# Attention scores with two stationary widths: 64 columns for the first 128 queries, 128 columns for the second

## What is computed

```
x = x + xattn(layernorm(x), ctx)          # x: 32 batches x 256 tokens x 256 features, ctx: 32 x 77 x 256
    q, k, v = heads(x @ Wq.T + bq), heads(y @ Wk.T + bk), heads(y @ Wv.T + bv)     # 8 heads of 32 features
    attn    = softmax(q @ k.T / sqrt(32) + causal)                                 # 256 x 77 per head
    out     = (attn @ v) @ Wo.T + bo
x = x + ffn(layernorm(x))
    h = silu(w1 x * s1) * (w2 x * s2);  h = gelu(h1 h * s);  h = gelu(h2 h * s);  out = w3 h * s   # 256 -> 1024 -> 1024 -> 1024 -> 256
```

## Time and profile before

| | |
|---|---|
| median of 3 runs | 1513.29 us (1512.74 to 1514.19) |
| the profiled execution | 1513.5 us, its span 1511.7 us |
| TensorE matmul busy | 1507.3 us (100% of the span), 8822 records |
| TensorE weight loads | 1201.6 us (79%) |
| VectorE / ScalarE / GpSimd | 841.7 us (56%) / 735.6 us (49%) / 115.1 us (8%) |
| granted TensorE clock | 1.000 |
| DMA | 92 GB/s mean |

### The profile page before, as it was taken

How to read it: one execution, slowest core, us unless ns; L and a number is a source line. 1 busy time by engine, 2 the same in 40 slices (tenths; PEclk the granted TensorE clock), 3 DMA queues, 4 the chain that set the end, 5 groups by cost and what they waited for, 6 DMA issues and landing times.

```text
span 1511.7 us, 22545 instructions
## 1 busy us (share of the span) xinstructions
PE 1507.3 (100%) x8822; PEld 1201.6 (79%) x8822; DVE 841.7 (56%) x1318; ACT 735.6 (49%) x1077; POOL 115.1 (8%) x119
## 2 busy tenths in 40 slices
PE   9999999999999999999999999999999999999999
PEld 6787887878878777887878878787887878878888
DVE  6754836458464564745548464574745648364432
ACT  5753635445363453635536364453634536354442
POOL 1001010010100101010010100101001010100000
PEclk9999999999999999999999999999999999999999
DMA  9962322233213222223223212322223223222100
GB/s 369 360 239 70 92 80 57 76 83 96 78 42 103 70 82 78 70 86 72 76 76 98 83 42 77 96 83 78 59 87 83 76 69 93 79 58 69 45 26 16
DMA packets 133747, 138.87 MB, mean 92 GB/s; under 512 B 74322, under 2 KB 105434, under 8 KB 130906
## 3 DMA queue, kind: packets, MB, share of 16 engines
q1 hardware_dynamic: 133722, 138.53, 30.4%
HBM read 78.70 MB, written 48.25 MB: 84 GB/s over the span
## 4 chain that ended last, share of the span: by engine, by line
PE 98%; DVE 1%; issue 0%; DMA 0%; SPq 0%; POOL 0%; DVEq 0%; POOLq 0%
PE ffn_banks L528 84%; PE att_banks L723 4%; PE att_banks L666 4%; PE att_banks L713 2%; PE att_banks L684 2%; PE ffn_banks L767 1%; PE ffn_banks L757 1%; PE ffn_banks L612 1%; DMA x_in<-in_x 0%; DVE a_f L970 0%; DVE probs L1030 0%; DVE a_lo L975 0%; PE att_banks L698 0%; PE att_banks L654 0%; DVE st L910 0%
## 5 line engine op out<-in xcount | busy, mean ns | idle before, releaser
L528 PE MATMUL ffn_banks<-b_hi,h_sb 128*128 128x512 f32 x1024 | 403.0, 394 | 0.0
L528 PE MATMUL ffn_banks<-b_lo,h_sb 128*128 128x512 f32 x1024 | 398.7, 389 | 0.0
L528 PE MATMUL ffn_banks<-a_hi,h_sb 128*128 128x512 f32 x1024 | 398.4, 389 | 0.0
L528 PE MATMUL ffn_banks<-a_lo,h_sb 128*128 128x512 f32 x1024 | 398.3, 389 | 0.0
L840 ACT ACTIVATE a_f<-ffn_banks,vec 128x512 f32<-128x512 f32 x128 | 88.3, 690 | 367.2 <-PE ffn_banks L528 367.2
L983 DVE TENSOR_TENSOR a_lo<-a_f,a_hi 128x512 fp32r<-128x512 f32 x128 | 103.9, 812 | 277.3 <-ACT a_hi L841 277.1
L528 PEld LDWEIGHTS ffn_banks<-b_hi,h_sb 128*128 128x128 f32 x1024 | 192.2, 188 | 45.6 <-issue 6.2
L528 PEld LDWEIGHTS ffn_banks<-a_hi,h_sb 128*128 128x128 f32 x1024 | 192.2, 188 | 39.9
L528 PEld LDWEIGHTS ffn_banks<-a_lo,h_sb 128*128 128x128 f32 x1024 | 192.2, 188 | 39.9
L528 PEld LDWEIGHTS ffn_banks<-b_lo,h_sb 128*128 128x128 f32 x1024 | 192.3, 188 | 39.4
L528 PE MATMUL ffn_banks<-ln_hi,w_sb 128*128 128x512 f32 x512 | 204.6, 400 | 0.4
(11 more groups left out here) (118 smaller groups left out, 1537.1 us busy)
## 6 DMA issues: line engine op xcount, KB each, us to landing
blocks_dram<-blocks SPq DMA_DIRECT2D x30, 512.0 KB, 3.1
attn_t<-blocks_dram SPq DMA_DIRECT2D x60, 256.0 KB
h_bits<-in_h SPq DMA_DIRECT2D x8, 1024.0 KB, 21.2
h_sb<-h_bits SPq DMA_DIRECT2D x8, 1024.0 KB, 9.9
x_in<-in_x SPq DMA_DIRECT2D x15, 512.0 KB, 3.6
ln_t<-in_x_t SPq DMA_DIRECT2D x15, 512.0 KB, 4.4
row_blocks_dram<-row_blocks SPq DMA_DIRECT2D x15, 512.0 KB, 4.1
row_blocks<-row_blocks_dram SPq DMA_DIRECT2D x60, 128.0 KB, 3.1
```

The lines of the kernel that those rows point to most:

```text
L528: mm = nc.tensor.matmul(psum, left, right, start=(k == 0 and part == 0), stop=(k == rows - 1 and part == 1))
```

## The change

`SCORE_COLS` becomes a pair, indexed by the half. The first 128 queries of a batch are scored as before, in 16 products of 64 stationary columns on eight tiles. The second 128 are scored in 8 products of 128 stationary columns, on four tiles of 32 rows by 128 columns. What is computed is the same.

```
-SCORE_COLS = 64
+SCORE_COLS = (64, 128)
...
                         for half in range(2):
                             for g in range(HG):
                                 at = half * G2 + g * TK
-                                for c in range(0, P, SCORE_COLS):
-                                    tokens = slice((2 * n + half) * P + c, (2 * n + half) * P + c + SCORE_COLS)
+                                for c in range(0, P, SCORE_COLS[half]):
+                                    tokens = slice((2 * n + half) * P + c, (2 * n + half) * P + c + SCORE_COLS[half])
                                     for h in range(4):
                                         rows = slice(HD * h, HD * (h + 1))
-                                        mm = nc.tensor.matmul(ab[c:c + SCORE_COLS, h, at:at + TK], q_t[rows, g, tokens],
+                                        mm = nc.tensor.matmul(ab[c:c + SCORE_COLS[half], h, at:at + TK], q_t[rows, g, tokens],
                                                               k_t[rows, g, n * TK:(n + 1) * TK], start=True, stop=True)
                         mm.then_inc(s_ready, 1)
```

## The result

The changed kernel takes 1515.85 us (median; 1515.31 to 1516.83) against 1512.95 us of the kernel before in the same runs: the ratio is 1.0018, 95% interval 1.0012 to 1.0024. The profiled execution has a span of 1513.7 us, against 1511.7.

The account below looks back on a forecast made before the run. TensorE, with a matmul under way 100% of the span, was taken as the bound. 32 score steps x 0.19 us = +6.1 us, other engines nothing, gave 1519.4 us against the median; range 1516.5 to 1521.5.

Parts of the forecast that it names:

- The first half: In each score step, the 16 products of 64 columns that are kept: 32 matmul records in 0.52 us.
- the switch: From 64 to 128 columns within a score step: array runs empty, first wide load 0.45 us after the step's start.
- the second half: Eight products of 128 columns on four tiles: loads in rounds 0.112 us apart, modelled end at 1.142 us.
- the end of the step: The product behind starts 0.07 us before the modelled end, at 1.07 against 0.89: 0.19 us more a step.
- The upper bound of the switch: Between 64 and 128 columns in a score step: the array runs empty; the lower bound was nothing.
- loads that wait for their own tile's stream: Rival, on the four wide tiles: a record takes 177 ns in place of 112; +12.3 us, 1525.8 us; chance 0.04.
- TensorE has no idle time to hide anything in: TensorE, 100% busy: whatever a score step gains or loses comes out of the total at full price, 32 times.
- item 4: ScalarE's copy and VectorE's mask behind S 0 have 2.2 us to spare, later products move back by 0.19: cost nothing.
- The last sentence: Sign of a wrong prediction: the step costs +0.19 us and the total doesn't follow, so TensorE had hidden slack.
- the first four cases: Slower by over 0.2%: forecast 0.79, no switch cost 0.09, load not hidden 0.04, loads in turn 0.01; given as 0.92.

Follow-up runs that it names:

- the kernel with three switches: The changed kernel with the width indexed by g, not the half (64, 128, 64, 128 in a step): 1526.91 us, ratio 1.0091 to the kernel before.

## Why the prediction was wrong

The direction was right; the size was not, and the fault lies outside the step.

- *The first half, the switch, the second half, the end of the step*: all held. 0.52, first wide load at 0.45, rounds of 0.112, product behind at 1.07, +0.184 against 0.19 forecast. The upper bound of the switch was the right end, and the kernel with three switches agrees with that price. So does the rule of the Trainium skill that the prediction set beside it ("TensorEngine Tiling (Array Packing)", "Key Properties"). No rival happened within the step: loads of a tile 0.112 apart leave no room for loads that wait for their own tile's stream, which would lie 0.177 apart.
- *"TensorE has no idle time to hide anything in"*, the first part's conclusion, is **the step that failed**. It took a matmul busy share of 100% for having no slack. A matmul's record lasts 0.39 while starts are 0.23 apart, so a wait of up to 0.16 between two products leaves no idle time in that row at all, and one of 0.25 hardly any. The loads' row showed it (6.1 us, 14 times), and so did the 1% of VectorE in the chain that the prediction quoted and passed over. 14 passes times 0.21 to 0.39, 3.9 us, are the missing term; the forecast's 6.1 less 3.9 is 2.2 and would have given 1515.5, beside a measured 1515.85.
- *"These engines lose no slack"*, item 4, looked at the copies behind S 0, which do have 2.2 us, and not at who holds the banks of L1 6. It also took for granted that all else moves back with TensorE. GpSimd's add does not: its DMA is issued 3.15 us behind the start of S 0 however long the step lasts, and VectorE is tied to the add. So VectorE's busy time did not stay unchanged, as forecast, but fell by 4.8 us.
- *The last sentence* named this way of being wrong ("slack that its 100% hides"), but no rival priced it.
- Two slips of arithmetic decide nothing: the chances of the first four cases add up to 0.93, not 0.92, and some rivals' times are counted from the profiled 1513.5, others from the median 1513.3.

## What to carry to other kernels

A TensorE that is 100% busy can still be waiting: read the starts of its matmuls, or the waits of its weight loads, before pricing an edit at full value. Time added on TensorE is free up to the wait that another engine imposes downstream of it, as long as that engine's work does not move back with it; and that wait can be the better thing to work on: here four pieces in place of one instruction on GpSimd bring 3.6 us, where the change to the scores cost 2.9. Here the narrow stationary operands were worth their instructions: with 64 columns the load (57 ns) is shorter than the stream (65), with 128 (112) it is not, both estimates of the prediction. And each further change of width in the middle of a step cost time.

## What the runs showed of the hardware

- GpSimd's add holds some of VectorE's instructions and not others. During it, a_f (line 970, one of its two tensors from PSUM, one from SBUF) took its usual 0.75, and a_lo (line 975, both from SBUF) waited for its end: 1.86 in place of 0.68. The Trainium skill, "SBUF — State Buffer", section "🔬 SBUF: two separate sides", says that an operation of VectorE with two SBUF inputs and a GpSimd operation that reads SBUF exclude each other for a whole instruction; the traces agree, in both directions, with 1.86 for 0.68 on VectorE and up to 1.94 for 0.73 on a piece of GpSimd's.
- Two more changes of width in a step, from 128 stationary columns to 64 and to 128 again on the same row groups, cost 0.35 us together (1.42 against 1.07 a step). What the single change costs was not measured by itself.
- In row tiles the loads hide behind the same tile's own stream, with 64 columns (0.30 from first to last start of 32 records) and with 128 (loads of one tile 0.11 apart, where a load of 112 ns and a stream of 65 in turns would make it 0.177; the two lengths are the prediction's estimates).
